# Last attention layer of a four-layer graph network: ELU's minimum on POOL, its sum first in the tick, head outputs moved by DMA into six full tiles

## The reference, cut to what matters

```python
def gat_layer(x, W, a_src, a_dst, bias, src, dst, heads, out_c, concat):
    h = (x @ W).reshape(n, heads, out_c)
    al_s = jnp.einsum('nhc,hc->nh', h, a_src)
    al_d = jnp.einsum('nhc,hc->nh', h, a_dst)
    e = jax.nn.leaky_relu(al_s[src] + al_d[dst], NEG_SLOPE)
    ...                      # softmax over the edges of each target node -> alpha
    out = jax.ops.segment_sum(h[src] * alpha[:, :, None], dst, num_segments=n)
    return out.reshape(n, heads * out_c) + bias

h = gat_layer(x, W1, a_src1, a_dst1, b1, src, dst, heads=8, out_c=96, concat=True)
h = jax.nn.elu(h)
out = gat_layer(h, W2, a_src2, a_dst2, b2, src, dst, heads=1, out_c=768, concat=False)
```

## Time and profile before

| | us |
|---|---|
| median of 3 runs | 1748.78 |
| the runs | 1748.78, 1748.90, 1743.21 |
| the profiled execution | 1743.84 |
| its span on the engines | 1742.0 |
| granted TensorE clock over the span | 0.944 |

### The profile page before, as it was taken

One profiled execution on the slowest core, in us unless ns is written; L12 is line 12 of the kernel. 1 busy time (PEld: TensorE's weight loads), 2 busy tenths in 40 slices (PEclk: granted clock), 3 DMA queues, 4 the chain that ended last, 5 costly groups with the idle time before them and its releaser, 6 DMA issues.

```text
span 1742.0 us, 26951 instructions
## 1 busy us (share of the span) xinstructions
PE 1521.1 (87%) x10142; PEld 1471.5 (84%) x10142; DVE 846.3 (49%) x2128; ACT 588.6 (34%) x1172; POOL 529.3 (30%) x681
## 2 busy tenths in 40 slices
PE   3978999997879999796999999999999998666777
PEld 3757989997879989786999999999999997566777
DVE  5886776316467753255533313141322225599643
ACT  3334444223344543222322232222232122366421
POOL 3244334232333332233213232323234231222222
PEclk9989999998989999987899999999999999868888
DMA  2222111122211111132112122112132222100012
GB/s 88 84 77 62 35 41 49 53 83 74 77 49 49 45 41 52 56 111 91 32 31 63 45 66 64 50 50 63 41 100 83 74 81 71 51 1 1 10 47 90
DMA packets 88125, 101.64 MB, mean 58 GB/s; under 512 B 9593, under 2 KB 80744, under 8 KB 87997
## 3 DMA queue, kind: packets, MB, share of 16 engines
q1 hardware_dynamic: 71986, 71.20, 14.1%
q10 hardware_dynamic: 16011, 28.73, 5.2%
HBM read 88.12 MB, written 11.78 MB: 57 GB/s over the span
## 4 chain that ended last, share of the span: by engine, by line
PE 60%; DVE 15%; issue 10%; ACT 6%; DMA 5%; POOL 3%; DVEq 1%; ACTq 0%; POOLq 0%; SPq 0%
PE ps L845 37%; PE ps L1025 7%; PE ps L1007 4%; PE ps L911 4%; DVE junk L1872 3%; DVE prob L1920 3%; DMA xl<-x_scratch 2%; PE ps L878 2%; DVE prob L1928 2%; PE ps L1069 2%; PE ps L1046 2%; ACT pairs L1237 1%; DMA xl<-in_x 1%; POOL pairs L1148 1%; DMA stage<-in_W 1%
## 5 line engine op out<-in xcount | busy, mean ns | idle before, releaser
L1148 POOL TENSOR_TENSOR pairs<-stage,pairs 128x256 fp32r<-128x256 f32 (+3 forms) x472 | 372.9, 808 | 791.1 <-ACT pairs L1237 789.8
L845 PE MATMUL ps<-pairs,XB 128*125 128x256 f32 (+2 forms) x2880 | 415.3, 304 | 26.4 <-issue 15.0
L845 PEld LDWEIGHTS ps<-pairs,XB 128*125 128x125 f32 (+1 forms) x2880 | 403.9, 192 | 30.1 <-issue 16.7
L845 PE MATMUL ps<-pairs,XA 128*125 128x256 f32 (+3 forms) x2655 | 374.1, 302 | 6.4 <-DVE XA L1558 2.3
L845 PEld LDWEIGHTS ps<-pairs,XA 128*125 128x125 f32 (+2 forms) x2655 | 368.2, 187 | 8.4 <-issue 2.9
L1237 ACT ACTIVATE pairs<-stage 128x256 fp32r<-128x256 f32 (+3 forms) x472 | 188.6, 423 | 506.0 <-PE ps L845 388.9
L1558 DVE TENSOR_TENSOR Hl<-ps,Hl 125x768 fp32r<-125x768 f32 (+3 forms) x57 | 43.6, 818 | 271.0 <-ACT Hl L1287 271.0
L911 PE MATMUL ps<-AT,Hg 125*128 125x314 f32 (+1 forms) x1080 | 165.7, 313 | 3.8 <-DVE rl L1956 3.8
L911 PEld LDWEIGHTS ps<-AT,Hg 125*128 125x128 f32 (+1 forms) x1080 | 160.7, 189 | 4.8 <-DVE rl L1956 3.7
L1195 POOL TENSOR_SCALAR prob<-prob,rden 125x625 f32<-125x625 f32 x80 | 70.9, 886 | 229.3 <-DVE rden L1936 229.3
L878 PE MATMUL ps<-ident,prob 125*125 125x125 f32 x475 | 85.3, 327 | 49.1 <-POOL prob L1195 18.6
(11 more groups left out here) (215 smaller groups left out, 1708.7 us busy)
## 6 DMA issues: line engine op xcount, KB each, us to landing
stage<-in_W SPq DMA_DIRECT2D x192, 128.0 KB, 2.3
stage<-in_rel SPq DMA_DIRECT2D x99, 192.0 KB, 2.4
stage<-in_root SPq DMA_DIRECT2D x91, 64.0 KB, 1.8
x_scratch<-xo ACTq DMA_DIRECT2D x15, 375.0 KB
xl<-x_scratch ACTq DMA_DIRECT2D x15, 375.0 KB
stage<-in_rel SPq DMA_DIRECT2D x42, 128.0 KB, 2.1
stage<-in_root SPq DMA_DIRECT2D x12, 192.0 KB, 2.4
stage<-in_W SPq DMA_DIRECT2D x12, 192.0 KB, 2.4
```

Source lines behind the costliest of these rows:

```text
L845: last = mm(o, X[:rows, xi, a, P * (s0 + t):P * (s0 + t) + m], pair(n, b), start=k == 0 and i == 0 and t * pitch % BANK == 0, stop=k == le ...
L1148: nc.gpsimd.tensor_tensor(pair(n, 1), staged(n), pair(n, 0).bitcast(F32), ALU.subtract).then_inc(*up("weights_lo", "weights lo", n))
```

## The change

- `elu` of layer 3: DVE's minimum is left out there, and POOL does it, behind its `softmax` rows in the same tick.
- `elu_sum` stands first in the tick at d = 2, ahead of `score_rows`. `elu_high` stands after `attention_T`, so ACT's row copy is ahead of it.
- Heads are written to slots 6, 7 and 8 of `XA` in turn. When a head's low part is done, SP moves its 96 rows by DMA (both parts) into tiles 0 to 5, where they fill 128 rows each; a head that crosses a tile's edge takes two DMAs. ACT waits for the move of head h - 3 before it writes a slot again.
- `project2` of layer 3 reads 6 tiles of 128 rows, waits for the moves of the two heads that end a tile, and W2 is loaded as 18 tiles of 128 by 256.

```diff
@@ gat_steps
         for t in range(heads * NT + 3):
             h, d = t // NT, t % NT
+            if h > 1 and d == 2:
+                yield ("elu_sum", l, h - 2, 0)
             if h < heads:
...
-            if h > 1 and d == 2:
-                yield ("elu_sum", l, h - 2, 0)
             if 0 < t <= heads * NT:
                 yield ("softmax", l, (t - 1) // NT, (t - 1) % NT)
-            if h > 1 and d == 2:
-                yield ("elu_high", l, h - 2, 0)
...
             if t >= 3:
                 yield ("attention_T", l, (t - 3) // NT, (t - 3) % NT)
+            if h > 1 and d == 2:
+                yield ("elu_high", l, h - 2, 0)
@@ weight_tiles, source, x2_place
-        rows = 128 if l < 3 else 96
+        rows = 128
...
-                    return [(XA, k, 96) for k in range(8)]
+                    return [(XA, k, 128) for k in range(6)]
...
-                return ("x2 lo", s[1], k) if s[1] == 3 else ("x2 lo", s[1], k // 4, k % 4)
+                return ("x2 moved", (128 * k + 127) // 96) if s[1] == 3 else ("x2 lo", s[1], k // 4, k % 4)
...
-                return XA, h
+                return XA, 6 + h % 3
@@ PE
                                     if ready != waited:
+                                        if ready[0] == "x2 moved":
+                                            pe.wait_ge(*at("x2 moved", 128 * k // 96))
@@ SP
+                if s[0] == "elu_high" and s[1] == 3:
+                    h = s[2]
+                    sp.wait_ge(*at("x2 lo", 3, h))
+                    f0 = 96 * h
+                    cut = min(96, 128 - f0 % 128)
+                    for p0, p1 in ((0, cut), (cut, 96)):
+                        if p0 < p1:
+                            r0 = (f0 + p0) % 128
+                            sp.dma_start(XA[r0:r0 + p1 - p0, (f0 + p0) // 128, :, :].bitcast(F32),
+                                         XA[p0:p1, 6 + h % 3, :, :].bitcast(F32)).then_inc(
+                                *up(f"x2_moved{h}", "x2 moved", h, by=16))
@@ POOL
+                elif kind == "elu" and s[1] == 3:
+                    n = agg_order[s[1:]]
+                    pool.wait_ge(*at("elu exp", n))
+                    nc.gpsimd.tensor_scalar(mn[:96, n % 2, :], mn[:96, n % 2, :], 1.0, -1.0, ALU.min, ALU.add).then_inc(
+                        *up("elu_min", "elu min", n))
@@ ACT, elu_high
                     act.wait_ge(*at("elu sum", n))
+                    if l == 3 and h >= 3:
+                        act.wait_ge(*at("x2 moved", h - 3))
@@ DVE, elu
+                    if l == 3:
+                        continue
                     dve.wait_ge(*at("elu exp", n))
                     V.tensor_scalar(mn[:m, n % 2, :], mn[:m, n % 2, :], 1.0, -1.0, ALU.min, ALU.add).then_inc(
```

More of the change, by code:

```diff
@@ L507, in build @@
                    "graph_out1", "graph_in", "degrees_out", "degrees_in"]
-                + [f"counts_back{d}" for d in range(NT)] + [f"counts_in{d}" for d in range(NT)])
+                + [f"counts_back{d}" for d in range(NT)] + [f"counts_in{d}" for d in range(NT)] + ["elu_min"] + [f"x2_moved{h}" for h in range(GAT_HEADS[3][0])])
         sems = {n: ctx.enter_context(nc.semaphore(n)) for n in names + dmas}
```

## The result

The changed kernel is slower. 13 runs have a median of 1754.49 us (1748.93 to 1758.43), 13 runs of the kernel before one of 1745.13 (1739.19 to 1751.36). The ratio is 1.0044, 95% interval 1.0029 to 1.0059. That is +7.7 us, the difference of the means (the medians are 9.4 apart), where -13.6 was forecast. The forecast of 1735.2 also started from the median of three runs, 1748.78, which stood 3.65 us above that of the 13; so part of its distance to the measured time lies in where it started, but not the wrong sign.

What follows compares the result with a forecast made beforehand. DVE was taken to bound the heads' periods, PE project2. -10.68 - 3.6 + 0.65 + 0 = -13.6 us, from the median of 1748.78 to 1735.2 us; range 1727 to 1742.

Steps and rivals of the forecast that it cites:

- What bounds the kernel: Layer 3's heads are bound by DVE (14.18 of 15.52 us), project2 by PE (42.73 of 42.73 us).
- Part 1: project2 with 6 tiles: 90 fewer matmuls at 0.1187 us each, all on the path, -10.68 us.
- Part 2: Five periods, heads of ticks h = 2 to 6: -0.72 us each, -3.6 us, between 0 and -5.2.
- POOL's minimum at 0.79 us, at most 1.50: Five periods: assumed duration, from POOL's one-input operation on 625 columns; upper bound from its two-input add, scaled.
- the wait of 1.05: Five periods: DVE's new wait for POOL's minimum before its sum, 1.05 us a head.
- POOL's rows stay at 0.79: Five periods: POOL's softmax rows keep taking 0.79 us; their overlap with score_rows costs DVE only 0.12.
- sum first and no gap shortens a period: Five periods: DVE's minimum (0.52 us) and its gap for ACT (about 1.35) go; a period is 14.8 instead of 15.5.
- rival of the eaten gain: Five periods: at a 1.50 us minimum DVE waits 1.76, nothing is won there; -9.1 in all, 1739.7 us; chance 0.14.
- Part 3: Last period (h = 7) and last sums: later POOL rows delay PE's transposes, +0.65 us, between 0 and +1.4.
- Part 4: Moves: the last, issued 4.45 us after project2's start x, takes 3.6 of 4.1 us allowed; stall 0, up to +2.5.
- estimate of 3.1 us: Last move inside SBUF: its time by the skill page's fit, beside the 3.6 us taken; the sum would stay.
- Part 5: Tail behind project2 (scores, five ticks, output loads): shifts as a whole, 0 us.

Runs made afterwards that it cites:

- e9: Changed kernel with the minimum back on DVE, and DVE's masked maximum of block 3 waiting for POOL's rows once a head: 1734.20 us, ratio 0.9927.
- e12: Changed kernel, POOL's minimum included, with DVE's masked maximum of block 3 waiting for POOL's rows once a head: 1749.47 us, ratio 1.0021.
- e3: Kernel before with only the DMA moves and six full tiles; minimum on DVE, order as before: 1736.71 us, ratio 0.9952.
- e5: Changed kernel with POOL's minimum replaced by multiplying by 1 twice, so the output is not the reference's: 1746.07 us, ratio 1.0000.
- e8: Kernel before with only DVE's sum moved to the start of its tick; ACT's order as before: 1743.46 us, ratio 0.9987.
- e7: Kernel before with only ACT's high half moved behind its row copy; DVE's order as before: 1746.83 us, ratio 1.0007.
- e4: Kernel before with only the new order: sum first in the tick, high half behind the row copy; minimum on DVE: 1751.94 us, ratio 1.0043.

## Why the prediction was wrong, point by point

- **What bounds the kernel: right.** The periods are DVE's, `project2` is PE's. Waiting put on DVE went straight into the period: from e9 to e12 the sum waits 2.47 us where DVE's minimum took some 0.5, and the period is 1.94 longer.
- **Part 1: right.** -10.68 us was forecast, and e3 has 270 matmuls in 32.11 us, -10.6.
- **Part 2: the step that failed.** It took -0.72 us a period, -3.6 for five; the changed kernel shows +0.65 in the first and +1.6 to +2.0 in the other four, +7.8 together. Two terms were wrong. *POOL's minimum at 0.79 us, at most 1.50*, was 2.30, and the wait of 1.05 was 2.47. I bounded the unknown by the nearest rows in size and number of inputs, and the pair of operations, which sets the price, was in neither bound; a row with another pair (L1206, 2.45 us) was in the trace. *POOL's rows stay at 0.79* stood in the sum unnamed: I charged their contest with DVE at 0.12 us on DVE's side and did not ask what it would be if POOL lost it. POOL lost it, at 2.2 to 2.96. Neither error alone makes the miss: with the price at 0.71 and the rows slow (e5) the ratio is 1.0000, with the rows quick and the price at 2.30 (e12) it is 1.0021, and with both gone (e9) 0.9927, -12.8 us. The mechanism of the part, that sum first and no gap shortens a period, was right: e8's periods are 14.4. That e9's are 14.7, where 14.8 was forecast, is chance, since it has DVE's own minimum and another wait in place of the 1.05. My rival of the eaten gain had the right mechanism and, from the same bound, too small a price. But carried on to 2.30 us its sum gives +4.0 in the periods, +2.2 in the last stretch and +1.0 of stall, -3.6 us in all, which is no slower kernel. What it lacked for the sign stands in e12, where the price is 2.30 and the rows are quick: +5.5 in the periods, but +7.3 in the last stretch.
- **Part 3: right in kind, far too small.** +0.65 us was forecast, at most +1.4. The last stretch grew by 9.0, from 30.85 to 39.87. By the runs: it is 34.48 us in e9, with order, moves and its one wait (granted clock 0.78 for 0.87), 38.12 in e12, with two minima of 2.30 on the path, and 39.87 with the late rows: 3.6 + 3.6 + 1.8. Of the first 3.6 up to 2.9 stand in e3 too, at the lower clock; the sum carried no term for the clock, and whether the edit sets it is open.
- **Part 4: the move somewhat short, its start wrong.** The moves of 471 KB take 3.7 to 4.2 us to landing for 3.6, and the last one, the one that counts, 4.2, just past the 4.1 that the sum left it. PE needs it at x + 8.70 (8.55 forecast), but SP issues at x + 6.02 instead of x + 4.45, since POOL's minimum stands ahead of it: 1.62 us of stall for 0. Without the minimum on POOL (e3) the move starts at x + 4.15, takes 4.0 and no stall comes. The prediction's estimate of 3.1 us, by a fit in the Trainium skill, "DMA: Bandwidth & Descriptors", section "Anatomy of one DMA — SWDGE (gpsimd) path", was 1.1 us short of the last move; the page gives that fit for DMAs issued from GpSimd, and the moves go by SP.
- **Part 5: right within 1.6 us.** The tail is 54.43 us in the changed kernel and 54.99 before; in e3 it was 53.40, which I haven't explained.

Added up, the parts alone give -8.4 + 12.8 + 7.5 = +11.9 us, and together they are +7.7. Of the 4.2 us of overlap e12 shows 2.8, as the slow rows cost 4.0 us beside POOL's minimum and 6.8 without it.

Open are three things: which operations of POOL are quick and which are not beyond the eight pairs, whether an edit sets the clock of the last stretch, and what decides at equal starts whether POOL or DVE gives way. Neither DVE's gap nor POOL's head start does (e7, e8). The place of ACT's high half does, since it is all that e4 has over e8, by a way that I can't see in the rows.

## What to carry to other kernels

Before work goes to POOL, find a row of POOL with the same pair of operations, not only the same size; a factor of three hides in the pair, and where there is no such row the upper bound must be far wider. If an instruction goes to an engine that another waits for, price also what that engine already does there: rows that have been quick can become more than three times as long when the order of other engines changes, here ACT's. And when several edits come together, time them apart: here one edit and a half of another gave -18.5 us, and the whole +7.7.

## What I had not expected of the hardware

- POOL's one-input instruction on 96 x 628 takes 0.71 us for mult+mult, mult+add and add+mult, and 2.30 to 2.34 for min+add, min+min, max+max, max+mult and add+add. DVE does min+add in 0.47.
- A POOL instruction of 0.79 us took up to 2.96 beside DVE's instructions with two SBUF inputs, one of 2.78 though it had started 0.53 us ahead of them; in another order with the same starts DVE lost 0.12 us instead. One row that DVE waited for, 0.32 us a head, kept all of the later ones quick.
- DMAs from SBUF to SBUF of 96 rows by 5,024 bytes landed in 3.7 to 4.2 us in the changed kernel, and pieces of a third of that still took 3.0 in the median.
